# Routing the tokens inside the attention slots, without PE's filler products

## What is computed

```
tokens = layernorm(patchify(5 shifts of x) @ W.T + b) * gamma + beta     # 32 x 36 x 192
h = concat(tokens, text_weight[x_txt])                                   # 32 x 68 x 192
pred = quantised(q) @ quantised(k).T ; idx = top_k(pred, 32)             # per head, 12 heads
h = h + proj(softmax(true_scores[idx]) @ v)                              # attention, keeps 32 of 68
x = layernorm(h)
w_f = top 4 of softmax((x @ W_fk + b_fk) @ emb_fk_n.T)                   # of 128 matrices 192 x 128
w_r = top 4 of softmax((x @ W_rk + b_rk) @ emb_rk_n.T)                   # of 128 matrices 128 x 192
hh  = sum over the 4 chosen f: w * (x @ f_know[f])
out = h + sum over the 4 chosen r: w * (hh @ r_know[r])
```

## Time and profile before

| | us |
|---|---|
| three runs | 987.29, 987.56, 990.06 (median 987.56) |
| profiled execution | 984.25, its span 982.4 |
| PE busy in the span | 794.3 |
| DVE busy | 677.0 |
| POOL busy | 553.8 |
| ACT busy | 324.5 |
| mean granted PE clock | 0.847 of 2.4 GHz |

### The profile page before, as it was taken

How to read it: one execution, slowest core, us unless ns; L and a number is a source line. 1 busy time by engine, 2 the same in 40 slices (tenths; PEclk the granted TensorE clock), 3 DMA queues, 4 the chain that set the end, 5 groups by cost and what they waited for, 6 DMA issues and landing times.

```text
span 982.4 us, 21622 instructions
## 1 busy us (share of the span) xinstructions
PE 794.3 (81%) x6343; PEld 643.7 (66%) x6343; DVE 677.0 (69%) x4161; ACT 324.5 (33%) x887; POOL 553.8 (56%) x764
## 2 busy tenths in 40 slices
PE   5789999999999999988662288899998699589800
PEld 3778888888888777755441266799976458455800
DVE  2199999999999999984788179885453254255423
ACT  0134334444444344434631011233321146434700
POOL 5256566665666565643547475004775777775075
PEclk9789889998999789975755579999997799889955
DMA  9233453534343346301372496456799798489533
GB/s 331 93 135 129 161 184 112 180 127 163 129 168 114 112 136 219 122 23 34 93 183 71 143 289 226 154 141 176 208 393 409 266 317 297 142 293 367 180 100 92
DMA packets 81578, 177.19 MB, mean 180 GB/s; under 512 B 12952, under 2 KB 38232, under 8 KB 78648
## 3 DMA queue, kind: packets, MB, share of 16 engines
q1 hardware_dynamic: 56088, 120.62, 37.1%
q10 hardware_dynamic: 14112, 32.12, 8.8%
q0 software_dynamic: 11264, 23.09, 7.6%
HBM read 94.25 MB, written 81.53 MB: 179 GB/s over the span
## 4 chain that ended last, share of the span: by engine, by line
DVE 34%; PE 28%; POOL 17%; issue 13%; DMA 5%; ACT 1%; SPq 1%; POOLq 0%; DVEq 0%; ACTq 0%
DVE work L1356 12%; DVE top L1350 9%; PE bank L1216 6%; POOL early L742 5%; PE bank L1199 4%; PE bank L1214 4%; POOL slots_g L749 3%; POOL slots_x L720 3%; PE bank L1264 3%; PE bank L1266 2%; DMA early<-slots_x 2%; DVE s_hit L1520 2%; PE bank L1250 2%; PE bank L965 1%; DVE place L1626 1%
## 5 line engine op out<-in xcount | busy, mean ns | idle before, releaser
L1356 DVE MATCH_REPLACE8 work<-top,work 128x68 f32<-128x68 f32 x896 | 179.3, 211 | 0.0
L1350 DVE MAX8 top<-work 128x8 f32<-128x68 f32 x896 | 128.9, 213 | 6.6 <-ACT tru L792 6.2
L1626 DVE COPY place<-bank 96x512 f32<-96x512 f32 x98 | 66.0, 685 | 82.3 <-PE bank L1199 81.6
L742 POOL DMA_INDIRECT early<-slots_h,s_all x68 | 65.6, 964 | 87.4 <-DMA slots_h<-m_y 67.0
L1635 DVE COPY place<-bank 128x256 f32<-128x256 f32 x98 | 40.9, 423 | 92.8 <-PE bank L1250 91.5
L965 PE MATMUL bank<-early,xp 128*128 128x192 f32 x432 | 94.0, 381 | 6.5 <-DMA xp<-in_a_x 5.0
L965 PEld LDWEIGHTS bank<-early,xp 128*128 128x128 f32 x432 | 90.5, 233 | 8.6 <-DMA xp<-in_a_x 5.3
L742 POOL DMA_INDIRECT early<-slots_y,s_all x68 | 66.3, 975 | 52.7 <-DMA slots_y<-m_y 30.5
L1199 PE MATMUL bank<-ident,early 128*96 128x128 f32 x392 | 68.2, 301 | 25.4 <-DMA early<-slots_x 25.4
L672 POOL TENSOR_TENSOR sc<-work,tru 128x476 f32<-128x476 f32 x32 | 38.0, 1189 | 87.5 <-ACT work L827 87.5
L720 POOL DMA_INDIRECT slots_x<-early,s_all x68 | 67.7, 996 | 31.6 <-issue 18.4
(11 more groups left out here) (187 smaller groups left out, 1729.5 us busy)
## 6 DMA issues: line engine op xcount, KB each, us to landing
early<-slots_x SPq DMA_DIRECT2D x49, 384.0 KB
slots_y<-m_y ACTq DMA_DIRECT2D x49, 384.0 KB
slots_h<-m_y ACTq DMA_DIRECT2D x49, 256.0 KB
early<-slots_g SPq DMA_DIRECT2D x49, 256.0 KB, 4.8
f_all<-in_f_know SPq DMA_DIRECT2D x16, 768.0 KB, 9.8
r_all<-in_r_know SPq DMA_DIRECT2D x16, 768.0 KB, 15.3
slots_x<-zero SPq DMA_DIRECT2D x28, 360.0 KB, 3.0
slots_x<-zero SPq DMA_DIRECT2D x28, 336.0 KB, 3.3
```

The source lines that it names most:

```text
L742: nc.gpsimd.indirect_dma_start(g_in[:, i % DEPTH, k, 0:width], None, src, bass.IndirectOffsetOnAxis(s_all[:, r - 1, i, k:k + 1], 0)).then_ ...
L1350: last = nc.vector.max(top8[:, c, :], work[:, par, c, :])
L1356: last = nc.vector.match_replace(work[:, par, c, :], top8[:, c, :], work[:, par, c, :], TAKEN)
L1626: nc.vector.tensor_copy(m_flat[u][0:HALF, :], turn_bank[u][0:HALF, :]).then_inc(sem["m_xt0"], 1)
```

## The change

Routing is moved into the slots. `LOAD_AT` gives the slot in which a tile is loaded: tile 0 in slot 18, tile 1 in 20, tiles 2 to 16 in slots 21 to 35. A tile takes four slots: load, statistics and root in slot b; normalising, transposes and query in b + 1; logits, choice, exponentials and one-hot in b + 2; position in b + 3. Slots 34 to 38 hold routing alone. To make PE free of patch products in most of them, all patch products are done eight a slot in slots 0 to 20, and `keep_busy` is gone. Each tile's products go to bank 7 or 3 in turn; the running place is no longer kept in PSUM: `t_position` adds the last row of the tile before with a float32 product (`first_row` times `place`) and one bf16 product. Part 0's counts and base are made in slots 31 and 32, its searches in slots 32 and 33, and its sends in slots 32 to 37 (`SEND_AT`: 3, 2, 1, 1, 1, 1 tiles). `find_slots` handles up to two tiles at once. `f_know` chunks 7 to 14 are loaded in slots 22 to 29, 0 and 1 after attention, 2 to 6 beside the first groups, 15 at group 7; part 0's groups run in the order 7 to 14, 0 to 6, 15, spill. The remaining searches are set beside the groups by hand, the last four of them in part 1's groups. The zeroing of the slot arrays is issued array by array.

The diff, cut to its core:

```diff
-FIRST, LAST = 4, 24
+FIRST, LAST = 4, 22
-LATE = 13
+LATE = 15
 for _n in range((PATCH_TILES - 2) * CHUNKS_K):
-    EMBED_AT.setdefault(_n // 8 if _n < 48 else 6 + (_n - 48) // 7, []).append((2 + _n // CHUNKS_K, _n % CHUNKS_K))
+    EMBED_AT.setdefault(_n // 8, []).append((2 + _n // CHUNKS_K, _n % CHUNKS_K))
+LOAD_AT = {18: 0, 20: 1, **{19 + _i: _i for _i in range(2, NT)}}
+ROUTED = max(LOAD_AT) + 4
+BASE_AT = 31
+FIND_AT = {BASE_AT + 1: ((0, 1), (1, 2), (3, 2)), BASE_AT + 2: ((5, 2), (7, 2))}
+SEND_AT = {BASE_AT + 1: (0, 1, 2), BASE_AT + 2: (3, 4), BASE_AT + 3: (5,), BASE_AT + 4: (6,), BASE_AT + 5: (7,), BASE_AT + 6: (8,)}
...
+            def t_position(i):
+
+                first = PARTS[part_of(i)][0]
+                at = routed_in(i)[:, 0:2 * NE]
+                pe.wait_ge(sem["t_hot"], i + 1)
+                pe.wait_ge(sem["t_exped"], i + 1)
+                if i > first:
+                    pe.wait_ge(sem["t_placed"], i)
+                    nc.tensor.matmul(at, first_row[:], place[:, :, i - 1], start=True, stop=False)
+                nc.tensor.matmul(at, lower_b[:], t_hot[:, i % 2].rearrange("p r n -> p (r n)"), start=(i == first), stop=True).then_inc(sem["t_pos"], 1)
...
             # PE's slot
                 if front:
                     queries_keys(b + 1, 1 - par)
+                if b - 2 in LOAD_AT:
+                    t_logits(LOAD_AT[b - 2])
+                if b - 3 in LOAD_AT:
+                    t_position(LOAD_AT[b - 3])
+                if b == BASE_AT:
+                    count_part(0)
                 if attended:
                     attend(b - 2, par)
                 if runs(b, 0, BATCH - 1):
                     values(b, par)
                 for t, k in EMBED_AT.get(b, ()):
                     embed(t, k)
-                if LAST_EMBED < b < BATCH:
-                    keep_busy()
+                if b - 1 in LOAD_AT:
+                    t_turn(LOAD_AT[b - 1])
                 if attended:
                     turn_out(b - 2)
                 if front:
                     scores(b + 1, 1 - par)
                 if attended:
                     project_out(b - 2, (m + 2) % 4)
+                if b - 1 in LOAD_AT:
+                    t_query(LOAD_AT[b - 1])
+                if b == BASE_AT:
+                    sum_counts(0)
+                if b == BASE_AT + 1:
+                    name_tiles(0)
...
             # DVE's slot
                 if take:
                     take8(b, par, 1)
+                if b - 2 in LOAD_AT:
+                    t_choose(LOAD_AT[b - 2])
...
                 if take:
                     take8(b, par, 2)
-                if embeds:
-                    embed_norm(NORM_AT[b])
+                if b in LOAD_AT:
+                    t_stats(LOAD_AT[b])
+                if b == BASE_AT:
+                    form_counts(0)
+                for i, n in FIND_AT.get(b, ()):
+                    find_slots(0, i, n)
...
             # POOL's slot, at its end
+                if b - 2 in LOAD_AT:
+                    t_one_hot(LOAD_AT[b - 2])
+                if b in LOAD_AT:
+                    t_rstd(LOAD_AT[b])
+                for i in SEND_AT.get(b, ()):
+                    send(i)
...
             # DVE, after attention
-            beside(turned_first, 0, range(NT + PARTS[1][1] - PARTS[1][0]), find)
-            beside(turned_first, 1, range(*PARTS[0]), first_sum)
+            for n in range(PART_GROUPS[0]):
+                turned_first(FIRST_GROUP[0] + n)
+                if n < 4:
+                    find_slots(0, PARTS[1][0] + 2 * n, 2)
+                if n == 4:
+                    form_weights()
+                if n in (6, 9, 12, 15, 18):
+                    first = (n - 6) // 3 * 2
+                    find_slots(1, first, min(2, PARTS[0][1] - first))
+
+            def sum_and_find(n):
+                first_sum(n)
+                if n % 2 == 0:
+                    find_slots(1, PARTS[1][0] + n, 2) if n < 8 else None
+
+            beside(turned_first, 1, range(*PARTS[0]), sum_and_find)
```

More of the change, by code:

```diff
@@ L432, in slot @@
                     load_residual(b, par)
+                if b in LOAD_AT:
+                    load_h1(LOAD_AT[b])
                 if b == 0:
@@ new lines, in t_query, with t_logits @@
+            def t_query(i):
+                pe.wait_ge(sem["t_xt"], i + 1)
+                for c in range(2):
+                    last = nc.tensor.matmul(routed_in(i)[:, 0:P], w_rt[:, c, :], t_xT[0:HALF, i % 2, c, :], start=(c == 0), stop=(c == 1))
+                last.then_inc(sem["t_qmm"], 1)
+            def t_logits(i):
+                pe.wait_ge(sem["t_qd"], i + 1)
+                nc.tensor.matmul(routed_in(i)[:, 0:2 * NE], t_q[:, i % 2], emb_t[:], start=True, stop=True).then_inc(sem["t_logit"], 1)
@@ L1182, in _ @@
-            route_in_turn(slot, t_step)
+                if b - 1 in LOAD_AT:
+                    t_query(LOAD_AT[b - 1])
[3 more added lines that the diff above has]
+                    name_tiles(0)
+            slots_of(pe, slot)
+            slot(BATCH + 1, 1)
+            for b in range(BATCH + 2, ROUTED):
+                if b - 2 in LOAD_AT:
+                    t_logits(LOAD_AT[b - 2])
+                if b - 3 in LOAD_AT:
+                    t_position(LOAD_AT[b - 3])
+                if b - 1 in LOAD_AT:
+                    t_turn(LOAD_AT[b - 1])
+                    t_query(LOAD_AT[b - 1])
@@ new lines, in form_base @@
+            def form_base(g):
+                st = part_steps[g]
+                first, end = PARTS[g]
+                mine = base[:, 2 * g:2 * g + 2]
+                nc.vector.tensor_copy(idf[:, first:end], idx[:, first:end, :, 0:K4])
+                dve.wait_ge(sem["base_products"], 3 * g + 2)
+                st.done(nc.vector.tensor_tensor(mine, bank_of_base(g)[:, 0:2 * NE].rearrange("p (q n) -> p q n", q=2),
+                                                iota_e[:].unsqueeze(1).to_broadcast([P, 2, NE]), ALU.subtract))
+                st.done(nc.vector.tensor_copy(ends[:, 2 * g:2 * g + 2], bank_of_base(g)[:, 2 * NE:2 * NE + 2]))
+                st.wait()
+                st.done(nc.vector.tensor_scalar(mine, mine, float(HALVED), float(HALVED * (NE - 1)), ALU.mult, ALU.add))
+                st.wait()
+                for q in range(2 * g, 2 * g + 2):
+                    last = nc.vector.tensor_scalar(ended[:, SPILL_AT[q]:SPILL_AT[q] + SPILLS[q]], iota_t[:, 0:SPILLS[q]], ends[:, q:q + 1], None, ALU.is_ge)
+                st.done(last)
```

624 lines of the change are left out of this document (282 added, 342 removed).

## The result

The changed kernel takes **1036.54 us** (median of 4 runs, 1020.94 to 1040.51) against 987.72 us (987.29 to 990.06) for the kernel before on the same chip: slower, at a ratio of **1.040, 95% interval 1.028 to 1.053**. The sign was forecast, the size was not: +40 to +49 us measured, +22 predicted, and the time lies outside the range of 964 to 1024.

The account below looks back on a forecast made before the run. No engine was taken to bound the whole span; DVE bounds ordinary attention slots, PE at 1.2 GHz some. Terms +68 + 2 - 54.5 + 6 = +21.5, taken as +22 on 987.56, gave 1010 us; own range 996 to 1024, overall 964 to 1024.

Parts of the forecast that it names:

- Part 1 and 2: Slots 18 to 31: routing adds DVE work, PE without fillers falls to 1.2 GHz; 235.5 against 167.2 us, +68.
- Rival (a): Attention slots: clock high for at least half of each slot, DVE bounds; -26, 962 us; chance 0.18.
- Rival (b): Attention slots: clock comes back in about every second slot; +45 there, about 985 us in all; chance 0.12.
- Part 3: Slots 6 to 20: eight patch products a slot instead of seven show where the clock dips; +2, bounds 0 and +5.
- Part 4: Slot 32 to first expert product: POOL's sends become the bound; 69.7 us for 124.3, -54.5, bounds -62 to -45.
- Rival (c): Tail: one-hots behind sends and DVE's searches lengthen each late slot 2 to 3 us; +10, no chance of its own.
- Part 5: Expert products: two-tile searches, +1 in part 0's groups and +5 in part 1's, together +6, bounds -3 and +14.
- Two thirds hidden: Part 1's expert groups: of 16 us of DVE work in four two-tile searches, two thirds hidden, giving +5.

Follow-up runs that it names:

- e10_after_again: The changed kernel run once more, unaltered: 1033.96 us, 1.035 of the kernel before.
- e1_fillers: The changed kernel with ten 512-column filler products put back into each of slots 21 to 31: 1010.12 us, 1.020 of the kernel before.
- e4_before_no_filler: The kernel before without its filler products (`keep_busy` calls, slots 24 to 31): 1007.73 us, 1.019 of the kernel before.
- e8_thin_fillers: `e3_both` with the same ten fillers a slot on 32 rows and 32 columns of the array instead of 128 and 128: 1058.69 us, 1.068.
- e2_single: The changed kernel with searches beside the expert products done one tile per group instead of two-tile searches: 1013.4 us, 1.026 of the kernel before.
- e9_stall_fillers: The changed kernel, two-tile searches kept, with 24 filler products behind each of part 0's nine groups that have a search: 1026.58 us, 1.037.
- e5_all_part0: `e3_both` with all 25 searches in part 0's 25 groups, one a group, none in part 1: 969.35 us, 0.979 of the kernel before.
- e6_before_pairs: The kernel before with its 25 searches done as pairs, two one-tile searches in a row in every second group of part 0: 1041.08 us, 1.052.
- e7_14_fillers: `e5_all_part0` with 14 filler products a slot instead of 10 in slots 21 to 31: 966.85 us, 0.977 of the kernel before.
- e3_both: The changed kernel with fillers back in slots 21 to 31 and one-tile searches beside the expert products: 986.66 us, 0.998 of the kernel before.

## Why the prediction was right in its sign and wrong in its size

**Part 1 and 2, the slots: right in the mechanism, the last microsecond by luck.** Predicted 235.5 us for slots 18 to 31, measured 234.5 in this profile, but 231.9 in `e10_after_again` and 226.8 and 226.7 in the two kernels with the same slots: the forecast was 1 to 9 us too high. In this profile seven of the eight slots 23 to 30 came out at 18.23 for 18.85, since routing's products took some 3.3 us at 1.2 GHz, not 3.9 (18.23 less 14.95), and slot 26 at 16.2; slots 22 and 31 were 17.2 and 15.3 for 16.4 and 17.4. That is 8 us too much forecast. It was made up by the slots 18 to 21, which took 13.4, 12.4, 18.5 and 13.9 for 50.9 in all: the clock was low in slot 20 already, one to two slots earlier than forecast. The deciding step, that fillers and not a busy PE give the clock back, was read from one stretch of 14 us and two places of the timeline; `e1_fillers`, `e4_before_no_filler` and `e8_thin_fillers` confirm it. Rival (a) needed mean slots below 16 us; they were 17.9 over slots 22 to 30. Rival (b), the clock back every second slot at half of the cost, came in part: in `e2_single` slots 24, 26 and 28 took 15.8 us, the mean over slots 22 to 30 is 17.3, and the stretch of 226.8 lies between its 212 and the forecast.

PE was busy for 22.80 of 22.80 us in a slot of `e8_thin_fillers`, and the granted clock was 0.50. By the Trainium skill's page "TensorE: Matmul & The Clock Gate", Part 1, sustained busy time releases the throttle; taken as busy time in the profile's sense, these runs disagree with it.

**Part 3, eight patch products a slot: +0.7 measured for +2.** Within its bounds of 0 and +5.

**Part 4, the tail: right.** 70.7 us measured, 69.7 predicted. Its working held too. The chain of work in order of time, over the last tile of part 0:

```profile
561.38 0.97 POOL slots_x L694
562.38 0.86 POOL t_hot L685
563.41 1.04 POOL slots_x L694
564.76 0.97 POOL slots_x L694
565.73 0.30 issue
566.04 0.97 POOL slots_x L694
567.01 0.30 issue
567.32 2.33 DMA slots_x<-early,s_all
569.66 3.26 DMA early<-slots_x
573.06 1.93 PE bank L1218 x8
```

Sends 1.28 us apart (once 1.35), a one-hot of 0.86 between them, landing 2.33 and first rows 3.26: the prices of the earlier trace rows. Rival (c) did not come, and the chain shows POOL, not DVE's two-tile searches in slots 32 and 33, setting the pace.

**Part 5, the searches beside the expert products: this step failed.** It said +1 in part 0's groups and +5 in part 1's, bounds -3 and +14; measured +16.0 and +25.7, a stretch of 463.2 us, over the 438 that the prediction named as its own refutation. The prediction counted DVE's microseconds and asked how many of them PE's work would hide. The count itself was sound: a two-tile search takes 4.36 us (605.55 to 609.91), the prediction had 4.0. What was missing is what such a stall does to PE. It had used the clock for slots of attention, where fillers stood, and did not ask the same of the products, where the row of 670.50 to 706.30 shows 1.00 with PE busy throughout and the copies of the earlier trace rows show one short search between two groups. The low stretch behind the pause of 2.46 us, 612.39 to 632.80, is 20.4 us long and holds seven steps of products that take 1.64 us each at 1.00, 11.5 in all: the 8.9 us more are far more than the pause. `e9_stall_fillers` shows it from the other side, with the stalls kept and the clock held. `e2_single` takes part 0's +16.0 back with the same searches in single tiles, `e5_all_part0` all but 4.1 us of part 1's 25.7 by taking the searches out of it, and `e6_before_pairs` puts 54 us into the old kernel without an added operation. "Two thirds hidden" for part 1, argued from DVE's idle 21 of 35.8 us, failed too: the idle time was there, but a search behind a sum still cost 1.5 us, 1.3 of them in a stretch at full clock, and how part 1's loss splits between these stalls and the low clock (0.79 for 0.95) is not shown.

Sum of terms against measured, in the spans: +68 for +67.3, +2 for +0.7, -54.5 for -53.6, +6 for +41.7, and the rest of the products, forecast unchanged, -2.3. One term carries the miss: with +41.7 in its place and the -2.3 the sum is +54.9, 1 us over the +53.8 between the two profiled executions (the medians are 48.8 apart). By the shorter slots of the other profiles the slots' term was 8 us too high as well, which hides part of the miss. The range was too narrow because its upper end gave part 5 at most +14, a bound from DVE's work alone.

**What the change is worth without its two faults.** The move of routing into the slots is sound: with fillers in and searches as single tiles in part 0, `e5_all_part0` takes 0.979 and `e7_14_fillers` 0.977 of the kernel before. Slots 18 to 31 then cost 203 to 205 us for 167.2, and the tail returns 53.

## What to carry to other kernels

Price a wait that you add to PE twice: its own length, and what the work behind it costs at half the clock; in part 0 eight more single searches of 2.7 us cost 1 us, and the same 25 in pairs cost 54. When you move work beside matrix products, spread it in the smallest pieces you have, and avoid two pieces behind one another where PE waits for the next copy. Products that compute nothing can pay for themselves: here those on the whole array did and those on a corner of it did not. Before you delete such a line run the kernel once without it and look at the granted clock, not at PE's busy share.

## What the runs showed of the hardware that was not expected

A pause of PE of 2.46 us, toward the end of 17 us at a granted clock of 1.00, was followed by 1.98-us rows within 2 us of its end, and the clock stayed at 1.2 GHz for 20.5 us in which PE was busy for 20.50. All seven falls behind the first rise in the products of this profile had such a pause, of 2.38 to 3.79 us, just ahead of them. The Trainium skill's page "TensorE: Matmul & The Clock Gate", section "HAM oscillation — how this bites in real kernels", has this mechanism for waits on DMA that are longer than the work between them. Here the wait was on a copy, and it was shorter than the 4.0 to 4.4 us of search that caused it.

The clock went with how much of the array the fillers used, not with PE's busy time, in the two kinds that were run: ten 512-column products a slot on 128 rows and 128 columns gave a granted clock of 0.89 over slots 18 to 31, the same ten on 32 and 32 gave 0.57, the changed kernel without any 0.59 to 0.61.

Kernels that do nearly the same work scatter very differently. The kernel before spread over 2.8 us in the first comparison (987.29 to 990.06) and 6 to 9 in the later ones, the changed kernel over 20 and 18 us, and with fillers `e1_fillers`, `e3_both` and `e5_all_part0` still over some 14 us. Often falling clocks alone do not explain it: `e6_before_pairs`, whose clock falls again and again in part 0, spread over 5.7 us, and `e7_14_fillers` over 3.4, in four runs each. Small differences between such kernels need many runs.
